# Layer norm columns at the first evictions and a new order of loads, roots, shifts and squares in the opening of a Perceiver layer

## The chip, the cores and the metric

The kernel runs on one core of a Trainium2 chip. The metric is the device time of one execution in microseconds (us). The engines are TensorE (PE), VectorE (DVE), ScalarE (ACT), GpSimd (POOL) and SyncE (SP). Each works through its own list of instructions in order; they meet through semaphores. Loads are issued by SP and by ScalarE and run on 16 DMA engines.

## The reference

One Perceiver layer: cross attention of 64 latent rows per batch (2 batches) over 1024 context rows, then self attention over the batch pair, then a gated feed-forward part. The part that matters here is the head of the cross attention.

```python
def layernorm(x, g, b, eps=1e-05):
    m = jnp.mean(x, axis=-1, keepdims=True)
    v = jnp.mean((x - m) ** 2, axis=-1, keepdims=True)
    return (x - m) / jnp.sqrt(v + eps) * g + b
xn = layernorm(x, ln_x_g, ln_x_b)               # context, 2 x 1024 rows of 256
ln = layernorm(latents, ln_l_g, ln_l_b)         # latents, 2 x 64 rows of 256
q = (ln @ Wq).reshape(b, m, h, d).transpose(0, 2, 1, 3)
kv = jnp.concatenate([xn @ Wkv, ln @ Wkv], axis=1)
...
qn = rmsnorm(q, qn_g) * scale
kn = rmsnorm(k, kn_g)
sim = jnp.einsum('bhid,bhjd->bhij', qn, kn)
```

All is fp32; 16 heads of 64. The latents are themselves the layer norm (without gain) of the layer's input.

## The kernel before

Rows are tiled by 128. The latents of both batches are one tile, the context is 16 tiles. The work before attention is a row of items: item 0 is the key projection of the latents, item 1 that of context tile 0, item 2 (`QI`) the query projection, and item i from 3 on the key projection of context tile i - 2. Items 0 to 9 (`ITEMS_A` = 10) and item 10's projection run ahead of the attention units; the other items are mixed into the units. Behind the items come 16 attention units and a tail, which the change doesn't touch.

The road of a context tile through the engines: SP loads it into one of four buffers of `raw`. VectorE takes its statistics (`tile_sums`, `tile_mv`; the lines 792 and 799). GpSimd forms the inverse root (`tile_rstd`, 425 and 426). VectorE centers and scales the tile in place (`tile_center`, 786). GpSimd multiplies by the gain row (`norm_scale`, 442) and adds the bias row (`norm_shift`, 449). ScalarE rounds it to fp32r (`context_high`, 542) and GpSimd forms what is left (`context_low`, 453). TensorE transposes it into PSUM (`norm_transposed`, 1075), ScalarE evicts it as fp32r (`xt_high`, 531) and VectorE forms the remainder (`xt_low`, 813).

A projection (`project`, 1122) has two halves of 512 columns; each is three pairs of matmuls, xth by wkh, xth by wkl and xtl by wkh, where wkh and wkl are the rounded weights and their remainder (628 on ScalarE, 886 on VectorE). The query projection is 8 fp32 matmuls (1107). After each half ScalarE squares the bank (`squares`, 548), VectorE sums by head (`key_norm2`, 818) and clamps (825), ScalarE takes the root (653), VectorE inverts it (910) and scales the keys (`key_scale`, 830), TensorE transposes them (`keys_transposed`) and ScalarE stores them (`keys_out`, 558 to 565). `project(i)` may not start before the keys of item i - 2 are scaled.

The latents: VectorE takes statistics of `xb` (782, 783), subtracts the mean and multiplies by the gain row `gl` (877), multiplies by the root and adds the bias row `bl` (880). TensorE transposes the result `lnf`. SP copies `lnf` to `lat2`, and ScalarE and GpSimd form `lnhl` from it (661, 501).

The order on each engine is written out by hand. SP's queue begins with xb, gl, bl, raw tile 0, the second half of `wraw`, the two context rows, raw tile 1, Wq, tiles 2 and 3, the row bout, the masks and four gain columns; each later tile waits for a shift. ScalarE issues the first half of `wraw`. `keep_clock` is a row of matmuls on the identity whose result isn't used (1229).

## Time and profile before

| what | value |
|---|---|
| median of 3 runs | 236.34 us (235.93 to 236.85) |
| profiled execution | 236.15 us |
| its span in the trace | 234.3 us |
| PE busy | 222.5 us, 95% of the span |
| DVE busy | 153.1 us, 65% |
| ACT busy | 151.7 us, 65% |
| POOL busy | 79.5 us, 34% |

Busy times of TensorE rest on modelled ends of matmuls, so its share isn't a share of its peak; the starts of its instructions are the better guide. In a row of the timeline the first number is the start in us from the span's start, the second the time covered, and the bracket gives the idle time before and what ended it.

### The profile page before, as it was taken

What the parts mean: (1) busy time and instruction counts of PE and PEld (TensorE: products, weight loads), DVE (VectorE), ACT (ScalarE), POOL (GpSimd) and SP (SyncE); (2) the same over time, 40 slices, a digit from 0 to 9 for tenths busy, and PEclk for the clock granted to TensorE, in tenths of its full rate; (3) what the DMA queues carried; (4) which work ended last, traced back from release to release, by engine and by line L of the source; (5) the groups of instructions that cost most, each with busy time, mean ns of one, the idle gap of its engine ahead of it and who ended that gap; (6) DMA issues with size and microseconds to landing.
All of it is one profiled execution on the core that took longest, in us unless ns stands there. A gap on an engine that the chain in (4) does not pass through costs nothing.

```text
span 234.3 us, 4173 instructions
## 1 busy us (share of the span) xinstructions
PE 222.5 (95%) x1449; PEld 193.2 (82%) x1449; DVE 153.1 (65%) x351; ACT 151.7 (65%) x331; POOL 79.5 (34%) x126
## 2 busy tenths in 40 slices
PE   7599999998999999999999999999999999899884
PEld 7365888885788989888898889899999988899773
DVE  1759999999886876768667655666766751304441
ACT  4235679988886769695867477787877765414251
POOL 5448867782383729273341500000000010000200
PEclk9859999999999999999999999999999999999999
DMA  5875110100000000000000699800000000000000
GB/s 177 300 227 192 45 49 25 42 28 22 0 22 3 0 6 0 0 0 3 0 3 0 217 413 340 203 0 3 1 3 0 0 4 0 0 3 0 0 3 22
DMA packets 11236, 13.80 MB, mean 59 GB/s; under 512 B 1584, under 2 KB 9936, under 8 KB 10960
## 3 DMA queue, kind: packets, MB, share of 16 engines
q1 hardware_dynamic: 10944, 13.01, 17.2%
q10 hardware_dynamic: 272, 0.52, 0.6%
q8 instruction: 12, 0.20, 0.3%
q14 instruction: 8, 0.07, 0.1%
HBM read 13.14 MB, written 0.13 MB: 57 GB/s over the span
## 4 chain that ended last, share of the span: by engine, by line
PE 70%; DVE 16%; DMA 3%; issue 3%; POOL 3%; ACT 3%; SPq 1%; POOLq 0%; ACTq 0%; DVEq 0%
PE banks L1208 19%; PE banks L1075 15%; PE banks L1122 10%; PE banks L1151 8%; PE banks L1341 5%; DVE small L818 4%; DVE sk L830 3%; PE banks L1222 3%; DMA rows<-in_L_xattn_ln_x_b 3%; PE banks L1153 3%; PE banks L1262 2%; DVE raw L786 2%; PE banks L1368 1%; DVE small L792 1%; PE banks L1399 1%
## 5 line engine op out<-in xcount | busy, mean ns | idle before, releaser
L853 DVE TENSOR_TENSOR ptl<-banks,pth 128x512 fp32r<-128x512 f32 (+1 forms) x48 | 26.8, 557 | 24.2 <-ACT pth L601 23.4
L1208 PE MATMUL banks<-xnh,pth 128*128 128x256 f32 x128 | 37.5, 293 | 0.0
L1208 PE MATMUL banks<-xnh,ptl 128*128 128x256 f32 x128 | 36.3, 283 | 0.0
L1208 PE MATMUL banks<-xnl,pth 128*128 128x256 f32 x128 | 36.2, 283 | 0.0
L548 ACT ACTIVATE sk<-banks 128x512 f32<-128x512 f32 x36 | 20.8, 605 | 16.4 <-PE banks L1122 15.9
L479 POOL TENSOR_TENSOR small<-small 128x16 f32<-128x16 f32 x7 | 20.4, 2915 | 32.4 <-DVE small L825 32.4
L601 ACT ACTIVATE pth<-banks 128x512 fp32r<-128x512 f32 (+1 forms) x48 | 23.7, 495 | 10.4 <-PE banks L1075 9.3
L818 DVE TENSOR_REDUCE small<-sk 128x8 f32<-128x512 f32 x36 | 23.6, 679 | 7.2 <-ACT sk L548 7.2
L830 DVE TENSOR_TENSOR sk<-banks,small 128x512 f32<-128x512 f32 x36 | 23.0, 679 | 6.5 <-POOL small L479 6.5
L459 POOL COPY sp<-sp 128x64 f32<-128x64 f32 x16 | 4.1, 256 | 63.7 <-ACT sp L582 63.4
L1208 PEld LDWEIGHTS banks<-xnh,pth 128*128 128x128 f32 x128 | 24.5, 192 | 0.4 <-issue 0.4
L1075 PE MATMUL banks<-ident,sp 128*128 128x128 f32 x144 | 24.2, 278 | 0.3 <-ACT sp L582 0.3
L1208 PEld LDWEIGHTS banks<-xnl,pth 128*128 128x128 f32 x128 | 24.5, 191 | 0.0
L1208 PEld LDWEIGHTS banks<-xnh,ptl 128*128 128x128 f32 x128 | 24.4, 191 | 0.0
L1122 PE MATMUL banks<-wkh,xth 128*128 128x512 f32 x68 | 23.4, 426 | 0.5 <-ACT xth L531 0.5
L582 ACT ACTIVATE sp<-sp,small 128x1088 f32<-128x1088 f32 x16 | 19.3, 1204 | 6.9 <-DVE small L842 6.5
L1122 PE MATMUL banks<-wkh,xtl 128*128 128x512 f32 x68 | 22.1, 407 | 0.7 <-DVE xtl L813 0.7
L1122 PE MATMUL banks<-wkl,xth 128*128 128x512 f32 x68 | 22.3, 410 | 0.0
L1075 PE MATMUL banks<-ident,sk 128*128 128x128 f32 x152 | 20.7, 274 | 0.6 <-DVE sk L830 0.6
L842 DVE CUSTOM_DVE_ANT_0 sp<-banks,mbias 128x1088 f32<-128x1088 f32 x16 | 20.5, 1280 | 0.0
L1075 PEld LDWEIGHTS banks<-ident,sp 128*128 128x128 f32 x144 | 16.4, 140 | 3.1 <-ACT sp L582 0.9
L1075 PEld LDWEIGHTS banks<-ident,sk 128*128 128x128 f32 x152 | 17.2, 140 | 2.0 <-DVE sk L830 1.2
(183 smaller groups left out, 477.0 us busy)
## 6 DMA issues: line engine op xcount, KB each, us to landing
knT<-in_L_attn_qkv_kernel SPq DMA_DIRECT2D x1, 3072.0 KB, 11.7
raw<-in_ctx SPq DMA_DIRECT2D x16, 128.0 KB, 2.0
knT<-in_L_xattn_Wq SPq DMA_DIRECT2D x1, 1024.0 KB, 9.0
wv<-in_L_xattn_Wkv SPq DMA_DIRECT2D x1, 1024.0 KB, 5.2
wout_sb<-in_L_xattn_Wout SPq DMA_DIRECT2D x1, 1024.0 KB, 5.6
knT<-in_L_attn_out_kernel SPq DMA_DIRECT2D x1, 1024.0 KB, 14.5
wraw<-in_L_xattn_Wkv ACTq DMA_DIRECT2D x1, 512.0 KB, 4.1
wraw<-in_L_xattn_Wkv SPq DMA_DIRECT2D x1, 512.0 KB, 6.0
```

Of the source, the lines that this page charges most:

```text
L479: nc.gpsimd.tensor_tensor(rn[:, i % 2, :], n2[:, i % 2, :], mhalf, ALU.pow).then_inc(rnp_ready, 1)
L548: nc.scalar.activation(sk[:, i % 2, h * 512:(h + 1) * 512], banks[:, k_banks(i) + h, :], ACT.Square).then_inc(sq_ready, 1)
L582: nc.scalar.activation(sp2[:, u % 2, 0:KW], sp2[:, u % 2, 0:KW], ACT.Exp, bias=nmax[:, u:u + 1], scale=-1.0, accum_out=rsum[:, u:u + 1]).t ...
L601: nc.scalar.activation(pth[:, j0:j1, :], banks[:, t3_bank(u, c), 0:(j1 - j0) * P].rearrange("p (j r) -> p j r", j=j1 - j0), ACT.Copy).then ...
L818: mark(nc.vector.tensor_reduce(n2[:, i % 2, 8 * h:8 * h + 8], sk[:, i % 2, h * 512:(h + 1) * 512].rearrange("p (h d) -> p h d", d=DH), AX. ...
L830: nc.vector.tensor_tensor(sk[:, i % 2, h * 512:(h + 1) * 512].rearrange("p (h d) -> p h d", d=DH), banks[:, k_banks(i) + h, :].rearrange(" ...
L842: nc.vector.tensor_tensor_reduce(out=sp2[:, u % 2, 0:KW], in0=logits_ps, in1=mbias[:, u // G, :], scale=-1.0, scalar=BIG, op0=ALU.add, op1 ...
L853: nc.vector.tensor_tensor(ptl[:, j0:j1, :], banks[:, t3_bank(u, c), 0:(j1 - j0) * P].rearrange("p (j r) -> p j r", j=j1 - j0), pth[:, j0:j ...
L1075: last = nc.tensor.transpose(dst[0:width, i * P:i * P + rows_], src(i), ident[0:rows_, 0:rows_])
L1122: last = nc.tensor.matmul(dst, a[:, n % 2, c, :], w[:, c, cols], start=(k == 0 and c == 0), stop=(k == 2 and c == DC - 1))
L1151: nc.tensor.matmul(dst, q_[:, u % 2, :], k_, start=(i == 0), stop=(i == 2))
L1208: nc.tensor.matmul(banks[:, u_bank(u), 0:D], p_[:, j, :], x_, start=(j == 0 and i == 0), stop=False)
```

## The change

Eight columns (gain and bias of the latents and of the context, two chunks of 128 each) are loaded into eight partitions by four small loads, transposed by TensorE into PSUM bank 6 and copied to `gcols`. The latents and context tile 0 are transposed centered and scaled only; gain and bias are applied when ScalarE evicts them, in `scaled`, one instruction for each chunk of 128 columns, once as fp32r and once as fp32 (`lnTf`, `x0Tf`). `xt_low` of these two reads the fp32 copy instead of PSUM. The gain and bias rows are still loaded, later, and `lnf` is formed on GpSimd in item 4. Tiles 1 to 3 are centered by ScalarE, with a product of mean and root from GpSimd (`nmr`). SP waits for the second weight half before the context rows and for two transposes before tile 4; bout, masks and gains go from tile 3 to tile 5, the copies to `lat2` from tile 4 to tile 10; `wv` is issued by ScalarE. In item 0's second half the wkl term comes last; item 1's terms are run as four and two pairs. The query evictions begin one item earlier, the `lnhl` copy five items later.

```diff
@@ SP
-            sp.dma_start(gl, row(ln_l_g)).then_inc(w_lrows, 16)
-            sp.dma_start(bl, row(ln_l_b)).then_inc(w_lrows, 16)
+            for i, v in enumerate((ln_l_g, ln_l_b)):
+                sp.dma_start(*gain_rows(i, v)).then_inc(w_cols, 16)
...
+                if k == 4:
+                    sp.wait_ge(xt_ps, 2)
                 sp.dma_start(raw[:, k % 4, :], ctx_tiles[k]).then_inc(w_ctx[k % 4], 16)
                 if k == 0:
                     sp.dma_start(wraw[:, :, 512:1024], wkv_v[:, :, 512:1024]).then_inc(w_k[1], 16)
+                if k == 1:
+                    sp.wait_ge(w_k[1], 16)
                     sp.dma_start(rows[:, 0, :], row(ln_x_g)).then_inc(w_rows, 16)
                     sp.dma_start(rows[:, 1, :], row(ln_x_b)).then_inc(w_rows, 16)
-                if k == 1:
+                if k == 2:
                     sp.dma_start(wq_sb, wq_v).then_inc(w_q, 16)
                 if k == 3:
+                    sp.dma_start(gl, row(ln_l_g)).then_inc(w_lrows, 16)
+                    sp.dma_start(bl, row(ln_l_b)).then_inc(w_lrows, 16)
+                if k == 5:
                     sp.dma_start(rows[:, 2, :], row(bout)).then_inc(w_bout, 16)
@@ GpSimd
+                if centered_by_act(k):
+                    link(last)
+                    last = nc.gpsimd.tensor_scalar(nmr[:, k % 4:k % 4 + 1], mv[:, k % 4, 0:1], -1.0, rstd[:, k % 4:k % 4 + 1],
+                                                   ALU.mult, ALU.mult)
...
+            tile_rstd(1)
             norm_scale(0)
             norm_shift(0)
-            tile_rstd(1)
...
+                if i < 2:
+
+                    norm_shift(i + 1)
+                    tile_rstd(i + 2)
+                    if i == 0:
+                        context_low(0)
+                    else:
+                        tile_rstd(i + 3)
+                    continue
...
+                if i == 4:
+                    pool.wait_ge(lat_hat, 1)
+                    pool.wait_ge(w_lrows, 32)
+                    link(nc.gpsimd.tensor_tensor(lmul, latg, gl, ALU.mult))
+                    nc.gpsimd.tensor_tensor(lnf, lmul, bl, ALU.add).then_inc(ln_ready, 1)
@@ ScalarE
+            for i, v in enumerate((ln_x_g, ln_x_b)):
+                act.dma_start(*gain_rows(2 + i, v)).then_inc(w_cols, 16)
...
+            def tile_center(k):
+                act.wait_ge(rstd_ready, k + 1)
+                nc.scalar.activation(raw[:, k % 4, :], raw[:, k % 4, :], ACT.Identity, bias=nmr[:, k % 4:k % 4 + 1],
+                                     scale=rstd[:, k % 4:k % 4 + 1]).then_inc(xhat_act, 1)
+
+            def scaled(dst, n):
+
+                for c in range(DC):
+                    g = 2 * DC * n + c
+                    last = nc.scalar.activation(dst[:, c, :], banks[:, t1_bank(n), c * P:(c + 1) * P], ACT.Identity,
+                                                bias=gcols[:, g + DC:g + DC + 1], scale=gcols[:, g:g + 1])
+                return last
...
+            act.wait_ge(cols_ps, 1)
+            nc.scalar.activation(gcols, banks[:, 6, 0:4 * DC], ACT.Copy).then_inc(cols_ready, 1)
+            act.wait_ge(cols_ready, 1)
+            act.wait_ge(xt_ps, 1)
+            scaled(xth[:, 0], 0).then_inc(xth_ready, 1)
+            scaled(lnTf, 0).then_inc(lnT_ready, 1)
             wk_high(1)
             squares(0, 0)
-            xt_high(1)
+            act.wait_ge(xt_ps, 2)
+            scaled(xth[:, 1], 1).then_inc(xth_ready, 1)
             squares(0, 1)
-            context_high(0)
+            scaled(x0Tf, 1).then_inc(x0T_ready, 1)
...
+                if i == 2:
+                    act.dma_start(wv[:, :, :], wkv_v[:, :, INNER:2 * INNER]).then_inc(w_v, 16)
...
+                if i == 2:
+                    tile_center(3)
                 act.wait_ge(n2_ready, i + 1)
                 nc.scalar.activation(sd[:, i % 2, :], n2[:, i % 2, :], ACT.Sqrt).then_inc(sd_ready, 1)
+                if i < 2:
+                    tile_center(i + 1)
+                if i == 0:
+                    context_high(0)
@@ VectorE
-            dve.wait_ge(w_lrows, 32)
-            nc.vector.scalar_tensor_tensor(latg, xb[:, :], lmv[:, 0:1], gl, ALU.subtract, ALU.mult).then_inc(lat_hat, 1)
-            dve.wait_ge(lat_hat, 1)
             dve.wait_ge(lat_rs, 1)
-            nc.vector.scalar_tensor_tensor(lnf, latg, lrs, bl, ALU.mult, ALU.add).then_inc(ln_ready, 1)
+            center(latg, xb[:, :], lmv[:, 0:1], lrs).then_inc(lat_hat, 1)
             tile_stats(0)
...
             wk_low(0)
+            xt_low(0)
             tile_center(0)
-            xt_low(0)
+            tile_stats(1)
             wk_low(1)
-            tile_stats(1)
             key_norm2(0, 0)
-            xt_low(1)
-            tile_center(1)
             key_norm2(0, 1)
...
                 if i == 0:
-                    tile_stats(2)
+                    xt_low(1)
+                if i <= 1:
+                    tile_stats(i + 2)
                 else:
                     tile_center(i + 2)
@@ TensorE
-            keep_clock(10, 7)
+            keep_clock(9, 3)
+            pe.wait_ge(w_cols, 64)
+            nc.tensor.transpose(banks[:, 6, 0:4 * DC], gb8, ident[0:4 * DC, 0:4 * DC]).then_inc(cols_ps, 1)
             norm_transposed(0)
-            for i in range(ITEMS_A + 1):
-                if i == 0:
-                    project(i, 0)
-                    project(i, 1)
-                if i > 0 and i + 1 != QI and i < ITEMS_A:
-                    norm_transposed(tile(i + 1))
-                if i >= 2:
+            keep_clock(2, 3)
+            project(0, 0)
+            project(0, 1)
+
+            for terms in ((0, 1), (2,)):
+                project(1, 0, terms)
+                project(1, 1, terms)
+            for i in range(2, ITEMS_A + 1):
+                if i == QI:
                     keys_transposed(i - 2, 0)
                     keys_transposed(i - 2, 1)
-                if i > 0:
-                    project(i, 0)
-                    project(i, 1)
+                if i < ITEMS_A:
+                    norm_transposed(tile(i + 1))
+                if i != QI:
+                    keys_transposed(i - 2, 0)
+                    keys_transposed(i - 2, 1)
+                project(i, 0)
+                project(i, 1)
```

## Rows read from the trace of the kernel before

**Rows 1.** The page, part 2: TensorE's granted clock in 40 slices, in tenths.
```profile
PEclk9859999999999999999999999999999999999999
```

**Rows 2.** Timeline of TensorE, 0 to 30 us: start, time covered, instruction.
```profile
1.69 4.64 PE L1229 MATMUL banks<-ident 128*128 128x128 f32 x20 [1.69 <-POOL ident L463]
7.61 0.41 PE L1075 MATMUL banks<-ident,knT 128*128 128x128 f32 x2 [1.28 <-DVE knT L880]
...
15.38 1.05 PE L1122 MATMUL banks<-wkh,xth 128*128 128x512 f32 x2
...
20.51 3.60 PE L1107 MATMUL banks<-knT 128*128 128x512 f32 x8
...
25.03 0.71 PE L1122 MATMUL banks<-wkh,xth 128*128 128x512 f32 x2
...
27.88 0.38 PE L1075 MATMUL banks<-ident,xn 128*128 128x128 f32 x2
```

**Rows 3.** Timeline of TensorE, 28 to 68 us.
```profile
51.15 1.03 PE L1075 MATMUL banks<-ident,sk 128*128 128x128 f32 x8
...
55.54 1.25 PE L1075 MATMUL banks<-ident,sk 128*128 128x128 f32 x8 [0.62 <-DVE sk L830]
```

**Rows 4.** Timeline of VectorE, 0 to 72 us.
```profile
6.46 0.48 DVE L877 SCALAR_TENSOR_TENSOR knT<-xb,small,knT 128x256 f32<-128x256 f32 x1 [2.22 <-DMA knT<-in_L_xattn_ln_l_b]
...
7.93 1.19 DVE L886 TENSOR_TENSOR wkl<-wraw,wkh 128x1024 fp32r<-128x1024 f32 x1
...
16.24 0.69 DVE L818 TENSOR_REDUCE small<-sk 128x8 f32<-128x512 f32 x1 [1.18 <-ACT sk L548]
...
17.86 1.29 DVE L830 TENSOR_TENSOR sk<-banks,small 128x512 f32<-128x512 f32 x2
...
53.05 1.41 DVE L786 TENSOR_SCALAR raw<-raw,small 128x256 f32<-128x256 f32 x1
```

**Rows 5.** Timeline of GpSimd, 0 to 66 us.
```profile
8.10 1.07 POOL L425 TENSOR_SCALAR small<-small 128x1 f32<-128x1 f32 x1 [2.94 <-DVE small L799]
...
11.08 1.24 POOL L442 TENSOR_TENSOR xg<-raw,rows 128x256 f32<-128x256 f32 x1 [1.11 <-DMA rows<-in_L_xattn_ln_x_b]
...
53.02 1.29 POOL L501 TENSOR_TENSOR lnhl<-knT,lnhl 64x512 fp32r<-64x512 f32 x1
```

**Rows 6.** Stretches: us, busy (count) PE PEld DVE ACT POOL, clock, DMA, GB/s.
```profile
6.40:10.30 3.90, 1.83 (x6) 0.80 (x6) 3.05 (x7) 1.61 (x3) 1.78 (x3) 1.00 0.81 245
...
10.40:13.80 3.40, 2.69 (x7) 1.78 (x8) 2.53 (x5) 0.60 (x1) 2.47 (x4) 0.50 1.03 386
...
219.00:222.00 3.00, 2.05 (x15) 1.53 (x15) 1.97 (x11) 0.68 (x2) 1.11 (x4) 1.00 0.00 0
```

**Rows 7.** DMA issues, 0 to 60 us: count, KB each, median us to landing.
```profile
raw<-in_ctx SPq DMA_DIRECT2D x15, 128.0 KB, 2.0
...
wv<-in_L_xattn_Wkv SPq DMA_DIRECT2D x1, 1024.0 KB, 5.2
...
wraw<-in_L_xattn_Wkv SPq DMA_DIRECT2D x1, 512.0 KB, 6.0
...
knT<-in_L_xattn_ln_l_b SPq DMA_DIRECT2D x1, 128.0 KB, 4.7
```

**Rows 8.** Timeline of SP's queue, 0 to 60 us: its issues.
```profile
2.55 0.43 SPq L369 DMA_DIRECT2D wraw<-in_L_xattn_Wkv  x1
...
6.69 0.81 SPq L375 DMA_DIRECT2D rows<-in_L_xattn_bout  x1
...
10.08 1.24 SPq L381 DMA_DIRECT2D small<-in_L_xattn_kn_g  x2
```

**Rows 9.** Groups by line and form, 0 to 60 us: count, busy us, mean ns.
```profile
L449 POOL TENSOR_TENSOR xn<-xg,rows 128x256 f32<-128x256 f32 x11 | 8.1, 738 | 0.1
...
L542 ACT ACTIVATE xnh<-xn 128x256 fp32r<-128x256 f32 x10 | 4.2, 420 | 0.0
...
L594 ACT ACTIVATE qh<-qbd 128x128 fp32r<-128x128 f32 x1 | 0.3, 293 | 0.0
```

More of the change, by code:

```diff
@@ L113, in perceiver_layer @@
         gl = early(4, 0, D)
+        gb8 = early(2, 0, P)[0:8, :]
+        lmul = early(2, D, D)
+        x0Tf = early(2, 2 * D, D).rearrange("p (c r) -> p c r", c=DC)
         bl = early(4, D, D)
@@ L116, in perceiver_layer, with centered_by_act, wait_centered @@
         wq_sb = knT[:, 1, 5:5 + DC, 0:INNER]
+        def centered_by_act(k):
+            return 1 <= k <= 3
+        def wait_centered(engine, k):
+            if centered_by_act(k):
+                engine.wait_ge(xhat_act, k)
+            else:
+                engine.wait_ge(xhat_ready, 1 if k == 0 else k - 2)
         def item(n):
@@ L142, in perceiver_layer @@
         mcol = small[:, 202:203]
+        gcols = small[:, 204:212]
+        nmr = small[:, 212:216]
         b0keys = knT[:, 0, :, :].rearrange("p g n -> p (g n)")
@@ L182, in perceiver_layer @@
         w_lrows = sem("w_lrows")
+        w_cols = sem("w_cols")
+        cols_ps = sem("cols_ps")
+        cols_ready = sem("cols_ready")
+        x0T_ready = sem("x0T_ready")
         z1_ready = sem("z1_ready")
@@ L485, in _ @@
                     norm_scale(i + 1)
-                if 0 < i <= B * NT:
+                if 1 < i <= B * NT:
                     context_low(i - 1)
-                if i + 2 < B * NT:
+                if i < 2:
[3 more added lines that the diff above has]
+                        context_low(0)
+                    else:
+                        tile_rstd(i + 3)
+                    continue
+                if 2 < i and i + 2 < B * NT:
                     tile_rstd(i + 2)
@@ L810, in xt_low @@
                 dve.wait_ge(xth_ready, n + 1)
+                full = banks[:, t1_bank(n), 0:D].rearrange("p (c r) -> p c r", c=DC)
                 if n == 0:
                     dve.wait_ge(lnT_ready, 1)
-                nc.vector.tensor_tensor(xtl[:, n % 2, :, :], banks[:, t1_bank(n), 0:D].rearrange("p (c r) -> p c r", c=DC),
-                                        xth[:, n % 2, :, :].bitcast(F32), ALU.subtract).then_inc(xtl_ready, 1)
+                    full = lnTf
+                if n == 1:
+                    dve.wait_ge(x0T_ready, 1)
+                    full = x0Tf
+                nc.vector.tensor_tensor(xtl[:, n % 2, :, :], full, xth[:, n % 2, :, :].bitcast(F32),
+                                        ALU.subtract).then_inc(xtl_ready, 1)
             def key_norm2(i, h):
@@ L911, in _ @@
                 rn_at = own[0]
-                if i > 0:
+                if i > 1:
                     tile_sums(i + 4)
@@ L1080, in norm_transposed @@
                     pe.wait_ge(consts, 1)
-                    pe.wait_ge(ln_ready, 1)
-                    src = lnf
+                    pe.wait_ge(lat_hat, 1)
+                    src = latg
+                elif n == 1:
+                    pe.wait_ge(xhat_ready, 1)
+                    src = raw[:, 0, :]
                 else:
@@ L1089, in norm_transposed, with project @@
                     pe.wait_ge(xtl_ready, n - 1)
-                    pe.wait_ge(lnT_ready, 1)
                 transposes(banks[:, t1_bank(n), :], lambda c: src[:, c * P:(c + 1) * P], DC).then_inc(xt_ps, 1)
-            def project(i, h):
+            def project(i, h, terms=(0, 1, 2)):
                 if i == ITEMS_A + 1:
@@ L1113, in project @@
                     pe.wait_ge(wk_hi, h + 1)
-                for k, (a, w) in enumerate(((xth, wkh), (xth, wkl), (xtl, wkh))):
-                    if k == 1 and i == 0:
+                order = ((xth, wkh), (xth, wkl), (xtl, wkh))
+                if i == 0 and h == 1:
+                    order = ((xth, wkh), (xtl, wkh), (xth, wkl))
+                for k in terms:
+                    a, w = order[k]
+                    if i == 0 and w is wkl:
                         if h == 1:
@@ L1118, in project @@
                         pe.wait_ge(wk_lo, h + 1)
-                    if k == 2:
+                    if a is xtl:
                         pe.wait_ge(xtl_ready, n + 1)
@@ L1123, in project @@
                                                 stop=(k == 2 and c == DC - 1))
-                last.then_inc(k_ps, 1)
+                if terms[-1] == 2:
+                    last.then_inc(k_ps, 1)
             def keys_transposed(i, h):
```

36 lines of the change are left out of this document (18 added, 18 removed).

## The prediction

> **What bounds the kernel now.** I read the page's second part first: TensorE is granted full speed everywhere except in the second and third of its 40 slices, 5.9 us each [rows 1]. So the start is odd, and the change only touches the start and the key items behind it. Next the TensorE timeline [rows 2]. After its 20 warming matmuls (1.69 to 6.33) TensorE waits 1.28 us for VectorE's latent norm and transposes at 7.61. It leaves item 0 at 15.38, starts the query projection (item 2) at 20.51 and item 3's key projection at 25.03. From then on it doesn't idle: the item that ends at 27.88 is followed by six more up to 51.15, 23.27 / 6 = 3.88 us each, until 55.54, where it waits 0.62 for VectorE's key scaling [rows 2, 3]. So items 3 to 10 run at TensorE's pace. Anything that makes TensorE start item 3 earlier moves the end by as much, unless another engine then falls behind; behind 55.54 nothing is changed but which moment things begin at.
>
> The start loses time in three ways. VectorE sits 2.22 us until the bias row of the latents lands, because gain and bias are applied before the transposes [rows 4]. GpSimd sits 1.11 us for the context bias row, and TensorE's tile 1 needs GpSimd's scale and shift first [rows 5]. And TensorE's clock: between 6.40 and 10.30 TensorE is busy 1.83 of 3.90 us, the clock then falls to 0.50 (1.2 GHz) and stays there into the third slice's end at 17.6 [rows 1], though TensorE is busy for 2.69 of the 3.40 us that follow [rows 6]. So item 0's second half and item 1 run at half speed.
>
> **The change, step by step.** All times below are on the profiled span.
>
> 1. Latents. xb lands as before; VectorE centers and scales in one instruction once GpSimd's root is there. The old pair waited for the bias row until 6.46 and released TensorE at 7.61. What stands late in SP's queue lands late: bias row 4.7 us from issue, second weight half 6.0 [rows 7]. I put the root at 5.2, the centering at 0.4 and the result at 5.6. TensorE's warming is 18 matmuls now, 18 × 4.64 / 20 = 4.2, to 5.87; then the new column transpose (0.2) and the latents' two (0.4, still slow): 6.6, against 8.0.
>
> 2. Evictions. ScalarE copies the eight columns out (0.2), then evicts the latents as two 128-column instructions with scale and bias instead of one copy. Bounds: 0.29 us for a 128-column copy, 0.42 for a 256-column one [rows 9]; I take the first, and some 0.2 from start to start. So xth at 7.25, the fp32 copy at 7.65, then the second weight copy (1.0, a little under VectorE's 1.19 for the same columns [rows 4]) to 8.6. Its data landed at 2.55 + 6.0 = 8.55 [rows 7, 8]; with two broadcast rows fewer ahead I take under 7.5, but if it lands as before everything behind it is 1 us later.
>
> 3. Item 0. TensorE: xth·wkh 7.35, wkl there at 7.35, xtl at 8.35, so h0 ends 8.8. h1 now runs its xtl term before wkl: to 9.75, then tile 0's transposes. VectorE: stats of tile 0 at once (raw tile 0 no longer lands behind the rows), wk_low(0) 6.15 to 7.35, xt_low, center(0) by 8.7, stats of tile 1, then wk_low(1) 9.25 to 10.45. GpSimd's small root is shut out meanwhile: the same root before wk_low took 1.07 instead of 0.2 [rows 5]. h1 ends at 11.0 against 15.38: 4.4 us ahead.
>
> 4. Item 1. Tile 0 goes through the columns too, so TensorE no longer waits for GpSimd's scale and shift. ScalarE evicts it at 10.7, squares h1 at 11.05 and gives the fp32 copy at 12.05. TensorE runs the four xth terms of both halves from 11.0 to 12.85 (8 matmuls at 2.85 / 12 = 0.24 [rows 2]). VectorE's second norm reduction starts at 11.65; before, it started at 16.24 and the scaled keys were out at 17.86 + 1.29 = 19.15, 2.91 later [rows 4]. xt_low(1) is inserted, 0.4, and it meets GpSimd's late scale and shift of tile 0 (11.45 to 12.95; GpSimd now does tile 1's root and its mean product first). Row for such a meeting: VectorE's centering took 1.41 instead of 0.4 under a GpSimd add of 1.29 [rows 4, 5]. Bounds 0 and 1.0; I take 0.4, as half of GpSimd's add is over when VectorE arrives. Item 1 ends on TensorE at 14.4 and item 0's keys are out at 15.35. The Trainium skill, SBUF — State Buffer, section "SBUF: two separate sides", says that VectorE takes the port pair that it shares with GpSimd also for an instruction with two SBUF inputs. xt_low(0) and (1) used to read a bank of PSUM, and both inputs are now in SBUF, so by that rule they are exposed where they were not; with the operand still in PSUM this step would be 0.4 us better. The root of 1.07 us under wk_low, which has two SBUF inputs, agrees with it.
>
> 5. Queries. TensorE transposes item 0's keys (0.8, to 15.8), tile 1's (0.25), and starts the query projection at 16.05 against 20.51. Its weights are issued behind the new wait for the second weight half and four more issues of 0.43 [rows 8], around 8.65, and the nearest 1 MB load took 5.2 [rows 7]: 13.9, two us early. It takes 3.45, to 19.5. The transposes of item 3 (0.2) and item 1's keys (0.8) give 20.5 against 25.03. **Lead 4.5 us.**
>
> 6. What must keep up until then. ScalarE centers tiles 1 to 3, three instructions whose nearest row is the 256-column copy of 0.42 (bounds 0.3 and 0.6, which move the end by nothing while the margins below hold) [rows 9]; each stands in front of GpSimd's scale of that tile. Tile 2: squares of item 1 15.0, context copy 15.4, root of item 1 16.9, centering 17.25; GpSimd scale and shift (0.74 each [rows 9]) to 18.8, needed at 19.5. Tile 3: ScalarE centers at 20.85 (behind two key evictions, the issue of wv, two squares and a copy), GpSimd's shift ends 23.1, needed at 23.35. Margin 0.25 only. VectorE is spared three centerings of 0.4; they pay for nothing while TensorE is the bound.
>
> 7. Queue of SP. The waits for the second weight half and for two transposes stand ahead of rows, Wq, all later tiles. Mask, bout and gains are moved from tile 3 to tile 5: 4.6 us of issuing, from 6.69 to 11.32 before [rows 8] and about 15.0 to 19.6 now, behind which tile 6 waits; it lands 2.0 after issue [rows 7], 21.6, and VectorE wants it at 22.25. Cost 0, bound 1 us if the tiny gain packets hold it: I take 0.1.
>
> 8. Items 3 to 9. GpSimd forms the latents' rows in item 4, two adds of 0.74, in what was its idle stretch; VectorE's centering falls into it and may wait 0.3 to 1.0. I take 0.3, since the port comes free between the two. The gain row, mask and query evictions on ScalarE are only shifted by one item; lnhl takes the place of a query eviction in item 8. The stall at 53.05 stays: GpSimd's 1.29 us instruction starts as far behind the tile before as it does now [rows 4, 5].
>
> Sum: 4.5 − 0.1 − 0.3 = 4.1 us. The span is 234.3 and the execution 236.15, so 1.85 lies around it; 236.15 − 4.1 = **232.05**, and as the profiled run is 0.19 under the median of 236.34 I say **232.1**.
>
> **The rivals.**
> - *The clock falls again (chance 0.2).* My schedule has no cover for a low clock. For: it stayed low through a stretch that was busy 2.69 of 3.40 us. Against: it fell only after 1.83 of 3.90; from 7 to 10.3 TensorE is now busy about 2.9 of 3.3, and late in the kernel it held full speed through 2.05 of 3.00 [rows 6]. A fall from 10.4 to 13.8 puts 0.24 on each of 12 to 14 matmuls, of which VectorE's work hides half: 1.5 us, **233.6**. The two rows against leave it 0.2. The Trainium skill, TensorE: Matmul & The Clock Gate, Part 1, says that the point of the change varies from run to run of one kernel; no row here can show that, and it would only make this case one of some runs rather than of all.
> - *The lead is spent in the items (0.1).* The 0.25 margin of tile 3, tile 6's landing and GpSimd's two adds each miss by their bounds (0.5, 1.0, 0.7): 4.5 − 2.2 = 2.3, **233.9**.
> - *Loads as before (0.06).* The weight half still lands at 8.55, or the four small column loads come late: 1 to 3 us of the lead never arise, 233 to **235.1**.
> - *More than forecast (0.1).* If VectorE's centering at the end of the items wins the port instead of losing it by 0.03 us [rows 4, 5], 1.0 less on VectorE, of which TensorE can use 0.62 [rows 3], plus the 0.4 not lost in steps 7 and 8: **231.1**.
> - *Slower (0.02).* The low clock lasts through the queries and item 3: 1.5, 3.45 and 2.85 on top of a lead of 4.5: −3.3, **239.5**. It decides from the point at which the low clock outlasts the query projection: 4.5 − 1.5 − 3.45 is −0.45.
>
> **How the numbers follow.** Forecast 0.52, the rivals as given. About 0.5% (235.2 to 237.5) is what can be told from no change. Faster takes the forecast and all rivals but the slow one and a third of the loads: 0.94; same 0.04; slower 0.02. The range goes from 230.9 to 234.5 and leaves out the last part of the loads, the slow case and some of the larger gain.
>
> **What would show it.** Latents' transposes at about 6.2; item 0 off TensorE at 11.0; query projection at 16 with 0.43 us per matmul; item 3's projection at 20.5; the last wait at 51.2 to 51.5 instead of 55.54; PEclk at full speed in the second and third slice. Wrong: PEclk of 0.50 behind 10 us; a TensorE idle stretch of over 1 us behind 20 us; VectorE centerings of 0.7 us and more in items 3 to 9.

## The result and the profile after

| | before | after |
|---|---|---|
| median of 7 runs each (lowest to highest), us | 236.34 (235.87 to 237.43) | 238.03 (236.71 to 239.14) |
| ratio after / before, 95% interval | | 1.0061 (1.0040 to 1.0082) |
| profiled execution, its span, us | 236.15, 234.3 | 238.03, 236.2 |

The changed kernel is 0.6% slower, where 232.1 us and a gain of 1.8% were forecast. The page's row of the granted clock and the head of its chain of work that ended last already say most of it.

```profile
PEclk9999889999999999999999999999999999999999
PE banks L1294 19%; PE banks L1153 16%; PE banks L1207 14%; PE banks L1237 8%; PE banks L1435 5%; DMA raw<-in_ctx 4%; PE banks L1308 3%; PE banks L1239 2%; PE banks L1356 2%; DVE small L900 2%; PE banks L1462 1%; SPq L413 1%; DVE sk L912 1%; PE banks L1493 1%; PE banks L1499 1%
```

Against [rows 1], the low slices moved from the second and third to the fifth and sixth (23.6 to 35.4 us), and a context load has 4% of the chain. The timeline of TensorE (start, time covered, instruction, idle time before it and its releaser) answers to [rows 2, 3]:

```profile
6.02 0.69 PE L1153 MATMUL banks<-ident,knT 128*128 128x128 f32 x2
...
11.42 0.74 PE L1207 MATMUL banks<-wkl,xth 128*128 128x512 f32 x2 [0.63 <-DVE wkl L965]
...
17.07 3.60 PE L1188 MATMUL banks<-knT 128*128 128x512 f32 x8
...
21.51 0.71 PE L1207 MATMUL banks<-wkh,xth 128*128 128x512 f32 x2
...
24.64 0.44 PE L1153 MATMUL banks<-ident,xn 128*128 128x128 f32 x2
28.09 1.95 PE L1153 MATMUL banks<-ident,sk 128*128 128x128 f32 x8 [3.01 <-DVE sk L912]
...
33.41 0.38 PE L1153 MATMUL banks<-ident,xn 128*128 128x128 f32 x2
...
56.93 1.22 PE L1153 MATMUL banks<-ident,sk 128*128 128x128 f32 x8 [0.51 <-DVE sk L912]
```

Read it as a balance of the lead over the kernel before, by the starts of the same instructions. The query projection starts 3.44 us early (20.51 to 17.07), item 3's projection 3.52 (25.03 to 21.51), item 4's first transposes 3.24 (27.88 to 24.64). So the start worked. Then TensorE sits 3.01 us, and the key transposes of item 4 (they are of the keys of item 2, the queries) begin at 28.09, which is to the hundredth when they began before: the lead is zero. From there to the transposes behind item 4 it takes 5.32 us (28.09 to 33.41) against 3.64 before (28.09 to 31.73), so the kernel is now 1.68 behind. The last wait of the items comes 1.39 late (55.54 to 56.93), and the span ends 1.9 late. Two losses made that: an idle stretch of 3.01, and the item behind it. The stretches (us, busy time and count of PE, PEld, DVE, ACT and POOL, granted clock, DMA share, GB/s) show what sort each is:

```profile
18.00:21.60 3.60, 3.60 (x18) 2.12 (x17) 3.50 (x11) 3.06 (x8) 2.93 (x7) 1.00 0.85 68
24.60:28.10 3.50, 0.45 (x3) 0.21 (x3) 1.09 (x3) 0.84 (x2) 3.11 (x7) 1.00 0.32 94
28.10:31.50 3.40, 3.40 (x12) 3.06 (x13) 3.40 (x10) 1.11 (x4) 0.81 (x3) 0.51 0.14 41
```

After 3.50 us in which TensorE was busy for 0.45, it is granted 0.51 (1.2 GHz) for 3.40 us, fully busy. What it had waited for stands in VectorE's timeline. VectorE runs its work in order, and the statistics of tile 6 stand in front of the scaling of the keys that item 4 transposes:

```profile
6.54 0.43 DVE L869 BATCH_NORM_STATS2 small<-raw 128x6 f32<-128x256 f32 x1 [1.20 <-DMA raw<-in_ctx]
...
13.88 0.41 DVE L895 TENSOR_TENSOR xtl<-knT,xth 128x256 fp32r<-128x256 f32 x1
...
22.26 0.82 DVE L863 TENSOR_SCALAR raw<-raw,small 128x256 f32<-128x256 f32 x1
...
27.01 0.43 DVE L869 BATCH_NORM_STATS2 small<-raw 128x6 f32<-128x256 f32 x1 [3.76 <-DMA raw<-in_ctx]
27.36 1.27 DVE L912 TENSOR_TENSOR sk<-banks,small 128x512 f32<-128x512 f32 x2
...
54.38 1.06 DVE L907 TENSOR_SCALAR small<-small 128x16 f32<-128x16 f32 x1
55.36 0.40 DVE L863 TENSOR_SCALAR raw<-raw,small 128x256 f32<-128x256 f32 x1
...
57.79 1.28 DVE L900 TENSOR_REDUCE small<-sk 128x8 f32<-128x512 f32 x2 [0.35 <-ACT sk L613]
```

Tile 6 was issued at 21.57 and landed 5.4 us later. SP's queue shows the block ahead of it (bout, masks, four gain issues: 16.72 to 21.52, against [rows 8]), ScalarE's queue shows the 1 MB of wv issued right beside it:

```profile
16.72 0.43 SPq L407 DMA_DIRECT2D rows<-in_L_xattn_bout  x1
17.20 0.91 SPq L409 DMA_DIRECT2D mask<-in_mask_BxS_bf  x2
18.15 1.71 SPq L413 DMA_DIRECT2D small<-in_L_xattn_qn_g  x2
19.90 1.62 SPq L413 DMA_DIRECT2D small<-in_L_xattn_kn_g  x2
21.57 17.56 SPq L394 DMA_DIRECT2D raw<-in_ctx  x5
```
```profile
17.87 0.40 ACTq L716 DMA_DIRECT2D wv<-in_L_xattn_Wkv  x1
```

And the list of DMA issues (count, KB each, median us to landing), against [rows 7]:

```profile
raw<-in_ctx SPq DMA_DIRECT2D x15, 128.0 KB, 2.4
...
wv<-in_L_xattn_Wkv ACTq DMA_DIRECT2D x1, 1024.0 KB, 8.3
```

wv took 8.3 us against 5.2, so it was in flight from 17.87 to 26.2, over all but the last 0.8 us of tile 6's landing (21.57 to 27.0). In the stretch from 18.00 the DMA engines are busy 0.85 of the time while moving only 68 GB/s.

### The profile page after: what moved, and what is told of

Read it like the earlier page. It is cut to its first block, busy times and chain, and to the rows that moved or that the text cites. A ratio compares the mean times of both kernels' runs of the same rounds, so it can differ in the third digit from the quotient of the medians.

```text
span 236.2 us, 4198 instructions
## 1 busy us (share of the span) xinstructions
PE 222.9 (94%) x1452; PEld 193.4 (82%) x1452; DVE 152.6 (65%) x347; ACT 155.4 (66%) x340; POOL 82.2 (35%) x131
## 3 DMA queue, kind: packets, MB, share of 16 engines
q1 hardware_dynamic: 10680, 11.97, 17.6%
## 4 chain that ended last, share of the span: by engine, by line
PE 74%; DVE 9%; DMA 4%; ACT 4%; issue 3%; SPq 2%; POOL 2%; ACTq 0%; DVEq 0%
PE banks L1294 19%; PE banks L1153 16%; PE banks L1207 14%; PE banks L1237 8%; PE banks L1435 5%; DMA raw<-in_ctx 4%; PE banks L1308 3%; PE banks L1239 2%; PE banks L1356 2%; DVE small L900 2%; PE banks L1462 1%; SPq L413 1%; DVE sk L912 1%; PE banks L1493 1%; PE banks L1499 1%
## 5 line engine op out<-in xcount | busy, mean ns | idle before, releaser
L613 ACT ACTIVATE sk<-banks 128x512 f32<-128x512 f32 x36 | 21.3, 602 | 14.9 <-PE banks L1207 14.3
L666 ACT ACTIVATE pth<-banks 128x512 fp32r<-128x512 f32 (+1 forms) x48 | 23.7, 495 | 10.4 <-PE banks L1153 9.3
L1153 PE MATMUL banks<-ident,sk 128*128 128x128 f32 x152 | 21.5, 282 | 3.7 <-DVE sk L912 3.5
L1207 PE MATMUL banks<-wkh,xth 128*128 128x512 f32 x68 | 23.1, 421 | 0.2
L1153 PEld LDWEIGHTS banks<-ident,sk 128*128 128x128 f32 x152 | 17.9, 144 | 5.5 <-DVE sk L912 5.1
L1207 PE MATMUL banks<-wkh,xtl 128*128 128x512 f32 x68 | 21.1, 394 | 0.4 <-DVE xtl L895 0.4
L1153 PEld LDWEIGHTS banks<-ident,sp 128*128 128x128 f32 x144 | 16.4, 140 | 3.1 <-ACT sp L647 0.9
```

The costliest lines, as they stand in the source:

```text
L613: nc.scalar.activation(sk[:, i % 2, h * 512:(h + 1) * 512], banks[:, k_banks(i) + h, :], ACT.Square).then_inc(sq_ready, 1)
L666: nc.scalar.activation(pth[:, j0:j1, :], banks[:, t3_bank(u, c), 0:(j1 - j0) * P].rearrange("p (j r) -> p j r", j=j1 - j0), ACT.Copy).then ...
L1153: last = nc.tensor.transpose(dst[0:width, i * P:i * P + rows_], src(i), ident[0:rows_, 0:rows_])
L1207: last = nc.tensor.matmul(dst, a[:, n % 2, c, :], w[:, c, cols], start=(k == 0 and c == 0), stop=(k == 2 and c == DC - 1))
```

## The experiments

**Which part holds tile 6.** Three theories: SP issues the tile too late (4.8 us of issuing ahead of it); the small packets of the gains hold it; or what bout and the masks put on the DMA engines, alone or with wv. First the whole block went back behind tile 3.

```
                 if k == 3:
                     ...
-                if k == 5:
                     sp.dma_start(rows[:, 2, :], row(bout))...
```

> The changed kernel with one edit undone: bout, the masks and the gain columns are issued behind tile 3 again, not behind tile 5. My theory: SP's 5.2 us of issuing (16.7 to 21.5) and the 5.4 us landing of tile 6 behind it made VectorE wait 3.76 us and TensorE 3.0 us, and the low clock (0.51 from 28.1 to 31.5) follows from that idle stretch. Then this run shows no wait of VectorE for tile 6, full clock behind 25 us, the lead of 3.5 us at item 3 kept, and 232.5 to 233.5 us. Rival 1, the lead is worth nothing because another engine holds the items anyway: 235.5 to 236.5 us, with idle TensorE in items 4 to 9. Rival 2, the block only moves the stall to tile 4, whose load is now behind it: a wait for tile 4 of 1 to 3 us and 234 to 236 us.

Measured: 234.05 us, ratio 0.9905 (0.9873 to 0.9937). No wait for tile 6, and the clock stays full. Its page and its timeline of TensorE:

```profile
PEclk9999999999999999999999999999999999999998
```
```profile
20.32 0.71 PE L1206 MATMUL banks<-wkh,xth 128*128 128x512 f32 x2
...
52.26 1.22 PE L1152 MATMUL banks<-ident,sk 128*128 128x128 f32 x8 [0.79 <-DVE sk L911]
```

Item 3 starts 4.7 us earlier than before, the last wait comes 3.3 earlier. So with the block at its old place the change gains 1%, though less than the 232.5 to 233.5 us expected. Of the 4.7, 1.2 isn't the block's: this execution was that much ahead of the changed kernel by item 3, and the first loads don't land alike in every execution (below). Next only the gains went back (this run was made last, behind the next three), and only bout and the masks:

```
 e2_gains_k3:  if k == 3: ..., gains       if k == 5: bout, masks
 e3_mask_k3:   if k == 3: ..., bout, masks if k == 5: gains
```

> The changed kernel with the four gain columns alone behind tile 3 again; bout and the masks stay behind tile 5 and wv stays with ScalarE. The run with bout and masks moved gave 234.1, that with wv moved 234.0. If the stall is made by all of it together (queue of SP and the 1 MB load beside it), taking the gains out is enough as well: tile 6 is issued by 19.7 and lands within 4 us, VectorE waits under 0.7 us, 233.7 to 234.5 us. If masks and wv on the DMA engines are what holds tile 6, it lands 5 us after issue, at 24.5 to 25, VectorE waits 1.5 to 2.5 us and the time is 235 to 236.5 us.

> The changed kernel with bout and both masks behind tile 3 again; the four gain columns stay behind tile 5. This parts the block. If the four gain loads (3.4 us of issuing, 6 to 7 us to landing each) are the cause, tile 6 is still late: issued around 19.8, landing at 24 to 25, VectorE waits 1 to 2 us, 234.5 to 236 us. If the masks are the cause, tile 6 lands before 23 and the time is that of the whole block undone (232.5 to 233.5 us).

With the gains back: 237.67, 1.0047 (1.0018 to 1.0075), though tile 6 was now issued at 19.56, 2.0 us earlier than in the changed kernel. It landed 7.1 us later, more than the 5 expected for the second theory, and VectorE (first fence) and TensorE (second) of that kernel wait as long as ever:

```profile
26.69 0.43 DVE L869 BATCH_NORM_STATS2 small<-raw 128x6 f32<-128x256 f32 x1 [3.94 <-DMA raw<-in_ctx]
```
```profile
27.76 1.71 PE L1153 MATMUL banks<-ident,sk 128*128 128x128 f32 x8 [3.18 <-DVE sk L912]
```

With bout and masks back: 234.12, 0.9919 (0.9886 to 0.9951). Tile 6, issued at 19.34, landed 3.6 later, and VectorE's wait is

```profile
22.93 0.43 DVE L869 BATCH_NORM_STATS2 small<-raw 128x6 f32<-128x256 f32 x1 [0.42 <-DMA raw<-in_ctx]
```

So neither the time that SP spends issuing nor the gains' packets are the cause. Tile 6 issued at 19.56 with the masks' loads just ahead takes 7.1, issued at 19.34 without them 3.6. Read alone, this says that masks and bout hold the tile. The next kernel tests whether the block costs that much by itself, in the kernel before, where wv is issued by SP: its block goes behind tile 5 as well, and GpSimd's product of the gains to item 3, so that it doesn't wait there.

```
-                if k == 3:
+                if k == 5:
                     sp.dma_start(rows[:, 2, :], row(bout))...
-                if i == 0:
+                if i == 3:
                     pool.wait_ge(w_gain, 64)
```

> The kernel before with nothing changed but the block: bout, masks and gain columns behind tile 5, and GpSimd's product of the gains in item 3 for it. My theory says the block costs what it costs wherever the tiles run: SP issues from 19.7 to about 24.5, tile 6 lands at 26.5 to 29 against VectorE's wish at 26.7, so 1 to 3 us and a possible fall of the clock: 237 to 240 us. The rival, that only the new start's earlier demand makes tile 6 late: 236 to 236.7 us, as before.

Measured: 236.18 against 236.28, ratio 0.9994 (0.9981 to 1.0008). Tile 6 was issued at 23.92, right behind the block, and landed 2.3 us later. The theory fell: the block at tile 5 costs nothing by itself. What differs is wv. Here SP issued it at 16.33, ahead of tile 5 and of the block, and 5.1 us later, at 21.4, it had landed; the masks were issued at 20.49, so the two met for 0.9 us only. In the changed kernel ScalarE issues it at 17.87, between masks and tile 6. So the block stayed and wv moved, to item 6:

```
-                if i == 2:
+                if i == 6:
                     act.dma_start(wv[:, :, :], ...)
```

> The changed kernel with the 1 MB load of wv issued by ScalarE in item 6 instead of item 2; the block stays. wv was issued at 17.9 and was on the DMA engines until 26.2, beside masks, gains and tile 6. If the landing of tile 6 (5.4 us from issue against 2.0 alone) is made by wv, tile 6 lands at 23.6 to 24.5, VectorE waits 0.4 to 1.2 us, TensorE under 1 us, the clock holds, and the time is 233.5 to 234.5 us. If SP's issuing or the gain packets alone make it late, the wait stays over 2.5 us and the time at 237 to 238 us.

Measured: 233.98, 0.9900 (0.9865 to 0.9935). Tile 6 was issued at 20.29, landed 2.3 later, and nobody waits for it. Of the block (its bout and masks) and wv either one may stay, not both:

| kernel | bout, masks issued | wv issued | tile 6 issued | to landing |
|---|---|---|---|---|
| changed | 16.7 to 18.1 | 17.87 | 21.57 | 5.4 |
| gains back | 16.2 to 17.6 | 17.36 | 19.56 | 7.1 |
| whole block back | 11.2 to 12.8 | 16.83 | 18.94 | 3.6 |
| bout, masks back | 10.4 to 12.0 | 17.13 | 19.34 | 3.6 |
| wv in item 6 | 16.4 to 17.7 | 35.73 | 20.29 | 2.3 |
| before, block at tile 5 | 20.0 to 21.4 | 16.33 | 23.92 | 2.3 |

wv itself lands 8.3 and 9.1 after issue in the first two rows and 5.1 to 5.6 in the others; the masks take 5.4 and 6.4 there, and 4.1 and 4.3 in the last two. That the two loads delay each other and the tile is shown. The traces also show when wv moved. ScalarE's queue carries nothing else in this time, so its megabytes in each stretch are wv's:

| kernel | 18 to 20 us | 20 to 22 | 22 to 24 | 24 to 26 | time of the 16 engines that SP's queue took, 18 to 20 |
|---|---|---|---|---|---|
| changed | 0 | 0.07 | 0.72 | 0.26 | 79% |
| gains back | 0 | 0.22 | 0.72 | 0.11 | 29% |
| bout, masks back | 0.39 | 0.66 | 0 | 0 | 2% |

With the masks just ahead wv, issued at 17.4 to 17.9, moves nothing for over 3 us, and then most of it moves beside tile 6. The 16 engines as a whole weren't full meanwhile: with the gains back they were busy 0.44 of the time from 17.4 to 21.0, and tile 6 took the longest there. Why wv stood still (which packets stand ahead of which on an engine) is not shown: no run looked into the queues of single engines.

**What the low clock costs.** TensorE of the changed kernel got 26 and then 17 matmuls of 128 columns, whose result nobody reads, into its wait at item 4 (each has two records in the trace).

```
+                if i == 4:
+                    pe.wait_ge(kt_ready, 4)
+                    for _ in range(17):
+                        nc.tensor.matmul(banks[:, 6, 384:512], ident[:, :], ident[:, :], ...)
```

> The changed kernel with 26 matmuls on the identity whose result is not used, in TensorE's wait of 3.0 us in front of item 2's keys; tile 6 stays late. It measures what the fall of the clock costs by itself. In the changed kernel the clock stood at 0.51 from 28.1 to 31.5, and the keys and the first half of item 4 took 3.4 us for what takes 1.9 elsewhere. My theory: the clock stays at full speed, and the time falls by 1.0 to 1.7 us to 236.3 to 237.0. Rival, the rest of the items is bound by VectorE's catching up behind tile 6, and the clock hides behind it: within 0.3 us of 238.0.

> As the filler run before, with 17 matmuls instead of 26. There the 26 ran from 24.4 to 30.2, some 1.5 us beyond the arrival of item 2's keys, so the clock held but the fillers themselves stood in the way, and the price of the clock was not shown. 17 take 3.8 us and end at about 28.2. Theory: the clock stays at full speed and the time is 236.3 to 237.2 us, 1 to 1.5 below the changed kernel. Rival, the clock's fall is hidden behind VectorE: 237.7 to 238.3 us.

With 26 they lasted until 30.2 and held TensorE up themselves: 238.34, 1.0091 (1.0066 to 1.0116), outside both expectations. That settles nothing. With 17: 237.44, 1.0034 (1.0015 to 1.0054), just beyond the theory's 236.3 to 237.2. The timeline of TensorE with 17 (first fence) and VectorE's wait for tile 6 (second):

```profile
23.70 3.96 PE L1338 MATMUL banks<-ident 128*128 128x128 f32 x34
...
28.79 1.25 PE L1153 MATMUL banks<-ident,sk 128*128 128x128 f32 x8 [1.14 <-DVE sk L912]
```
```profile
27.72 0.43 DVE L869 BATCH_NORM_STATS2 small<-raw 128x6 f32<-128x256 f32 x1 [5.69 <-DMA raw<-in_ctx]
```

The clock stays full in every slice. Tile 6 was later still here, so I compare from VectorE's statistics of it: to the end of item 4 it takes 4.93 us (27.72 to 32.65) against 6.40 (27.01 to 33.41). The low clock costs 1.5 us at item 4. By the last key transposes 0.8 of it is left (29.09 against 29.92), and in the runs 0.6 (238.03 to 237.44, with intervals that overlap). The runs' own list has a second witness. One of the seven of the changed kernel had a mean granted clock of 0.998 (the others 0.986 to 0.993); it took 236.71 us, 1.3 under the median of the other six. With the gains back one had 0.999 and took 236.03, 1.7 under the other six. Neither has a trace, and their wait for tile 6 may have been shorter as well, so 0.6 to 1.7 is as well as the price is known. Either way, without the fall of the clock the changed kernel would still not be faster: the late tile alone eats the lead.

This pair also shows how far single executions differ at the start. Up to item 4 both run the same instructions; item 3's projection begins at 20.23 with the 17 matmuls and at 21.51 without, where tile 0 had landed 3.8 and 4.7 us after its issue.

**The rest of the gap, and a better version.** The three kernels without the late tile end near 234.0, not 232.1. The next ones start from a kernel in which the gains go out while SP waits for the second weight half, the masks stay behind tile 5, bout goes behind tile 12 and wv into item 6.

> The changed kernel with the block taken apart: the gain columns are issued in SP's wait for the second weight half, the masks stay behind tile 5, bout goes behind tile 12, and wv is issued by ScalarE in item 6. My theory: all tiles land in time, no wait of VectorE for a load behind 10 us, and the lead at item 3 (3.5 us) arrives at the end of the items as 3.3: 233.0 to 233.8 us. Rival, the four gain loads slow the second weight half, which lands at 7.9 us now: item 0 gets later by as much as it does, 0.5 to 1.5 us, and the time is 234.3 to 235.3 us.

Measured: 234.02, 0.9915 (0.9893 to 0.9937), no better than the simple ones and beyond the theory's 233.8. Its VectorE timeline shows where it still loses:

```profile
26.61 0.82 DVE L864 TENSOR_SCALAR raw<-raw,small 128x256 f32<-128x256 f32 x1 [0.64 <-POOL small L458]
...
50.35 1.06 DVE L908 TENSOR_SCALAR small<-small 128x16 f32<-128x16 f32 x1
51.33 0.40 DVE L864 TENSOR_SCALAR raw<-raw,small 128x256 f32<-128x256 f32 x1
```

At 26.61 tile 5's centering waited for GpSimd's root. At 50.35 a clamp of 16 columns takes 1.06 instead of 0.17, and it is the centering behind it that is short; before it was the other way round [rows 4, 5]. The changed kernel has the same, at 54.38, and its GpSimd timeline shows what the clamp meets:

```profile
54.13 1.28 POOL L551 TENSOR_TENSOR lnhl<-knT,lnhl 64x512 fp32r<-64x512 f32 x1
```

ScalarE's root, mask row, key evictions and squares hang on the clamp. So GpSimd was made to wait with lnhl until tile 11 is centered:

```
                     pool.wait_ge(xn_ready, i + 2)
+                    wait_centered(pool, ITEMS_A + 1)
                     nc.gpsimd.tensor_tensor(lnhl[M:P, :, :], ...)
```

> The kernel of the run before this one, and GpSimd's instruction for lnhl waits until tile 11 is centered. In the changed kernel this GpSimd instruction (1.28 us) started 0.25 us before VectorE's clamp of item 9, which took 1.06 us instead of 0.17, and ScalarE's root, mask, key evictions and squares of item 10 all came behind the clamp. Before the change it was the centering behind the clamp that was held. My theory: with the wait the clamp takes 0.2 us and the centering 0.4 us, the keys of item 9 are out 0.6 to 0.9 us earlier, VectorE's wait for the squares of item 10 goes, and the time is 0.7 to 1.2 us below the run without it. Rival, TensorE is the bound there and hides it: the same time within 0.2 us.

Measured: 233.25, 0.9878 (0.9854 to 0.9901), 0.77 better than without the line. (In the two traces the last keys come 1.14 earlier, 0.25 of it there by item 3 and 0.88 from the clamp on.) Its VectorE timeline (first fence), and TensorE's at the last keys, which wait no more (second):

```profile
50.09 0.17 DVE L909 TENSOR_SCALAR small<-small 128x16 f32<-128x16 f32 x1
50.18 0.41 DVE L865 TENSOR_SCALAR raw<-raw,small 128x256 f32<-128x256 f32 x1
```
```profile
51.76 1.23 PE L1155 MATMUL banks<-ident,sk 128*128 128x128 f32 x8
```

Then the start: tile 0 lands 4.0 to 4.7 us after its issue, beside the second weight half. Here SP issues that half only once tile 0 is there.

```
                 if k == 0:
+                    sp.wait_ge(w_ctx[0], 16)
                     sp.dma_start(wraw[:, :, 512:1024], ...)
```

> The kernel of the run before this one, and SP waits for raw tile 0 before it issues the second weight half. In the changed kernel tile 0 landed at 6.5 us, 4.7 after its issue, though nothing but small loads stood ahead of it, and VectorE waited 1.2 us for it. If the second weight half, issued 0.4 us behind, shares its engines and slows it, tile 0 lands at 4.5 to 5.3 us, item 0's second weight split is then late instead (the half lands at 8.5 or later, against 7.9), and the time moves by less than 0.5 us either way. If the first weight half on ScalarE's queue is what slows it, tile 0 still lands at 6 to 6.5, the weight half at 9 or later, and the time is 1 to 1.5 us more.

Measured: 233.70, 0.45 worse than without it. Tile 0 landed at 5.1, 3.3 after issue, but the weights at 9.0 instead of 7.7, and TensorE then sits 1.16 us for their high part (10.21). Both are wanted at once, and the other order was the dearer one. Last, the two meetings left in items 3 to 5: GpSimd forms tile 5's root first in item 3, and, on top, waits with its two adds for the latents until tile 6 is centered.

```
+                if i == 3:
+                    tile_rstd(5)
...
                 if i == 4:
+                    wait_centered(pool, 6)      (second kernel only)
                     pool.wait_ge(lat_hat, 1)
```

> The fastest kernel so far (block taken apart, wv in item 6, lnhl behind tile 11's centering; 233.25 us), and GpSimd forms the root of tile 5 first in item 3 instead of behind two adds. In that kernel the statistics of tile 5 were there at 21.4 but the root came at 26.3, VectorE waited 0.64 us for it and its centering then took 0.82 instead of 0.41, and TensorE's keys of item 3 came about 0.3 us late. Theory: VectorE's wait goes, item 3's keys are out 0.5 to 0.9 us earlier, and the time is 0.3 to 0.7 us less, 232.5 to 233.0 us. Rival, the centering then meets GpSimd's next add on the shared port and loses as much: 233.0 to 233.4 us.

> The kernel of the run with tile 5's root first (233.07 us), and GpSimd's two adds for the latents' rows in item 4 wait until tile 6 is centered. In that kernel VectorE's centering of tile 6 took 0.89 instead of 0.41 us under the first of them, and TensorE then waited 0.44 us for item 4's keys. Theory: the centering takes 0.4, TensorE's wait goes, and 0.3 to 0.5 us is gained, 232.6 to 232.8 us. Rival, the adds now delay GpSimd's scale of tile 6 and the root of tile 7 and the centering of tile 7 waits instead: 233.0 to 233.3 us.

First kernel: 233.07, 0.9860 (0.9844 to 0.9877), the same as 233.25 within what these runs tell apart, as the rival had it. The wait for the root is gone, and in its place the clamp there takes longer. The timeline of its VectorE:

```profile
25.52 0.67 DVE L911 TENSOR_SCALAR small<-small 128x16 f32<-128x16 f32 x1
...
30.49 0.89 DVE L867 TENSOR_SCALAR raw<-raw,small 128x256 f32<-128x256 f32 x1
```

Second kernel: 234.25, 0.9921 (0.9892 to 0.9950), so over 1 us worse, beyond both expectations (0.4 of it is in its trace by item 3 already). Tile 6's centering falls from 0.89 to 0.40, but GpSimd is then late with the next root, and both come back one item on, in that kernel's VectorE:

```profile
35.19 0.82 DVE L868 TENSOR_SCALAR raw<-raw,small 128x256 f32<-128x256 f32 x1 [0.55 <-POOL small L458]
```

The fastest version is the first, 233.07 us: 1.4% under the kernel before and about 2% under the changed one (ratios 0.9860 and 1.0061 to the same kernel before).

## Why the prediction was wrong

The predicted sign was wrong, and one step made it so: step 7. The other misses together were about 2 us: with either of the two loads moved the kernel takes 234.0 and not 232.1.

**The low clock at the start doesn't show in the time.** The prediction counted the low clock of items 0 and 1 among the three losses. (Item 1's second half already ran at full speed: from 17.57 a pair of matmuls took 0.46 from start to start, as in item 3.) With the experiments the kernel before was run 45 times more, with the mean granted clock of each. In 23 it is 0.983 to 0.985, as in the profiled one, and they took 236.04 to 236.74 us, median 236.43. In 11 it is 1.000, and they took 236.36 to 237.00, median 236.63; the fastest were six at 0.993, 235.31 to 235.42. So full clock from the start didn't make that kernel faster, and what the changed kernel gains there isn't shown to come from the clock. Why is open, since none of the 11 left a trace.

**Steps 1 and 2 held within 0.6 us.** The latents' transposes start at 6.02 and are over at 6.71 (forecast 6.6), TensorE's first projection starts at 7.67 (7.35), the second weight half is copied from 8.20 (7.65). A pair of 128-column evictions took 0.81, where 0.29 each and 0.2 from start to start were put.

**Step 3 missed a landing.** It let tile 0 land early because the rows no longer stand ahead of it. It landed 4.7 us after issue, at 6.5, and VectorE waited 1.20 for it. So the low part of the first weight half started at 7.10 and not 6.15, that of the second at 10.17 and not 9.25, and TensorE left item 0 at 12.0 and not 11.0. The run with the weights held back shows one part of why: without the second half beside it the tile took 3.3 and not 4.0 to 4.7. What keeps it above 2.0 there isn't shown; the first half, on ScalarE's queue, was in flight in all of them.

**Step 4's meeting went elsewhere.** xt_low(1) took 0.41, without a hold; the clamp just ahead of it took 0.41 instead of 0.17. In none of the traces is xt_low(0) or (1) held (0.41 to 0.43 us), so no run shows that having both inputs in SBUF costs them anything.

**Step 5 held from there.** From the query projection to item 3's projection it took 4.44 us (forecast 4.45), and the lead was 3.5, in the other kernels with this start 3.9 to 4.8, against 4.5. **The rival of a clock that falls again** at 10.4 to 13.8 did not come there: the clock is full to 23.6 us. It came behind tile 6, for another cause: the mechanism was on the list, the idle stretch that set it off was not.

**Step 6: the margin was overdrawn.** Tile 3's centering started at 21.51 (20.85). GpSimd's shift of it, forecast to end at 23.1, started only at 23.85, behind tile 4's root, its own scale and the remainder of tile 2 (22.90 to 23.69), which the step left out:

```profile
23.85 0.74 POOL L485 TENSOR_TENSOR xn<-xg,rows 128x256 f32<-128x256 f32 x1 [0.17 <-POOL xnl L489]
```

From item 3's projection to tile 3's transposes it is 3.13 us (21.51 to 24.64) and was 2.85 (25.03 to 27.88), so 0.3 of the lead goes there, in every kernel with this start. Tile 5's root was late by 0.64 once nothing else was in the way, because GpSimd had not caught up; the step ended its account at tile 3.

**Step 7 is the one that failed.** It counted SP's issues nearly right (4.8 us against 4.6; 16.7 to 21.5 against 15.0 to 19.6 with the later start) and set tile 6's landing to 2.0 us, where it took 5.4. The 2.0 was a median over 15 tiles, most of them issued later, without such loads beside them [rows 7]. Its one reason for a delay was the gains' small packets, and the run with them moved away shows the tile as late as ever. And the prediction costed the move of wv as a ScalarE issue only, not as 1 MB on the DMA engines beside the masks. Priced at 0.1 with a bound of 1, it cost 3.24 of lead by 28.09, of which 3.01 as an idle TensorE, and 1.68 behind that, 1.5 of it by the clock: 4.9 in all. With either load moved it costs nearly nothing, 233.98 to 234.12 us. Its own rival "the lead is spent in the items" had tile 6 in it, at 1.0.

**Step 8: right place, wrong size, and the wrong claim about the end.** In the kernels without the late tile, tile 6's centering meets the latents' adds and takes 0.89 to 0.90, so 0.5 over its 0.4 and not 0.3. (In the changed kernel it is the clamp ahead of it that meets them, 0.38 instead of 0.17.) "The stall at 53.05 stays" failed: GpSimd's instruction now meets the clamp and not the centering. Before, only VectorE was held and ScalarE's chain went on; now that chain is held too. From the clamp to item 10's norm reduction it is 3.41 us (54.38 to 57.79) and was 3.04 (52.97 to 56.01), and with lnhl held back it is 2.53. The 0.37 more is most of the 0.5 lost behind the last wait, and the 0.88 between 3.41 and 2.53 is what the lnhl experiment brought (0.77 in its runs). "Behind 55.54 nothing is changed" was wrong for the same reason.

**In sum.** The best version is 3.2 us under the kernel before (236.28 and 236.45 to 233.25 and 233.07), against the 4.1 of the sum. In the trace of the 233.07 kernel the lead over the kernel before is 4.28 us at item 3's projection (forecast 4.5). At tile 3 0.3 goes, at item 6 0.75, behind tile 6's held clamp and centering (the prediction put 0.3 there), and 0.15 elsewhere; 0.7 comes back at the last key transposes (51.75), where TensorE no longer waits, and 0.4 goes right behind them, where it waits for VectorE anew. Its TensorE timeline shows both waits:

```profile
32.46 1.26 PE L1157 MATMUL banks<-ident,sk 128*128 128x128 f32 x8 [0.44 <-DVE sk L916]
...
56.11 0.41 PE L1157 MATMUL banks<-ident,xn 128*128 128x128 f32 x2 [0.47 <-DVE sk L916]
```

That leaves 3.4 at 56.11, and the span is 3.3 shorter. Two sums of the prediction are also off by a little: 232.05 and 0.19 are 232.24 and not 232.1, and the chances that it adds up for "faster" come to 0.96 and not 0.94.

## What to carry to other kernels

A median landing time holds for the load on the DMA engines under which it was read. When a load moves, draw what is in flight during its old and its new place on all queues, also those of other engines, and price the first tile behind by a row read under a like overlap. A load that arrives late under a TensorE bound can be paid twice, as here: as 3.0 us of idle time, and then as a low clock for the item behind it. And where one engine's long instruction locks another out, the moment of the meeting decides who pays: a held instruction with no dependant is cheap, the clamp 0.1 us ahead of it, on which a third engine waits, is not.

## What the runs showed of the hardware

While broadcast loads of bout and two masks and a 1 MB load of another queue were in flight together, the DMA engines of the changed kernel were busy 0.85 of the time and moved 68 GB/s; late in item 0 the same engines moved 314 GB/s at 0.95, in this stretch of the changed kernel:

```profile
10.40:13.80 3.40, 2.77 (x13) 1.94 (x11) 2.50 (x4) 2.10 (x5) 3.13 (x5) 1.00 0.95 314
```

A 128 KB tile issued behind the two took 5.4 us there and 7.1 with the gains back, where the engines were busy 0.44 and moved 120 GB/s from 17.4 to 21.0; in the kernels in which the two loads hardly met it took 2.3 to 3.6. Under GpSimd's instruction of 1.3 us even a VectorE instruction of 16 columns, 0.17 us long, took 1.06. The Trainium skill, SBUF — State Buffer, section "SBUF: two separate sides", tells of such a lock between the two engines, and this row agrees with it. The clock stayed full through a stretch in which TensorE was busy 2.77 of 3.40 us and fell after one of 0.45 of 3.50.
